# A decoder's latent attention: masking the diagonal blocks of the scores by a VectorE addition in place of TensorE products

## The reference

```python
kv_d = x @ kv_d_w;  q_d = x @ q_d_w
k = concat([(kv_d @ k_u_w), rope(x @ rope_k_w)])       # per head
q = concat([(q_d @ q_u_w), rope(q_d @ rope_q_w)])
v = kv_d @ v_u_w
scores = einsum('bqhd,bkhd->bhqk', q, k) / sqrt(32)
scores = where(tril(ones((256, 256))), scores, finfo.min)
out = einsum('bhqk,bkhd->bqhd', softmax(scores), v)
h = x + out.reshape(b, s, 512) @ o_w
```

## Time and profile before

| what | value |
|---|---|
| time, median of 3 runs | 2256.36 us (2255.92 to 2256.59) |
| profiled execution: its span, the only time shown of it | 2257.6 us |
| PE busy | 2145.6 us, 95% of the span |
| PEld busy | 1788.6 us, 79% |
| DVE busy | 1307.3 us, 58% |
| ACT busy | 1078.4 us, 48% |
| POOL busy | 677.1 us, 30% |

### The profile page before, as it was taken

One profiled execution on the slowest core, in us unless ns is written; L12 is line 12 of the kernel. 1 busy time (PEld: TensorE's weight loads), 2 busy tenths in 40 slices (PEclk: granted clock), 3 DMA queues, 4 the chain that ended last, 5 costly groups with the idle time before them and its releaser, 6 DMA issues. The chain is left out here.

```text
span 2257.6 us, 43111 instructions
## 1 busy us (share of the span) xinstructions
PE 2145.6 (95%) x17918; PEld 1788.6 (79%) x17918; DVE 1307.3 (58%) x2283; ACT 1078.4 (48%) x1887; POOL 677.1 (30%) x684
## 2 busy tenths in 40 slices
PE   6999998899999999999999999999799999899996
PEld 5666666444489999999999999999677877799995
DVE  7666776689854445444544444454555455767764
ACT  4676633478744444333433344333455554425553
POOL 4111210266512221111111111211255543125664
PEclk9999999999999999999999999999999999999998
DMA  7454202100032222321223123221000000258995
GB/s 261 160 170 134 81 11 113 57 1 1 29 131 108 89 100 106 112 75 64 86 94 113 64 87 119 79 70 49 25 2 2 2 2 30 85 187 262 275 274 103
DMA packets 46931, 215.30 MB, mean 95 GB/s; under 512 B 6161, under 2 KB 6161, under 8 KB 32401
## 3 DMA queue, kind: packets, MB, share of 16 engines
q1 hardware_dynamic: 29968, 139.13, 17.1%
q0 software_dynamic: 16768, 73.41, 11.3%
HBM read 169.00 MB, written 43.52 MB: 94 GB/s over the span
## 5 line engine op out<-in xcount | busy, mean ns | idle before, releaser
L336 POOL TENSOR_TENSOR c_prob<-c_prob,c_inv_mass 128x512 f32<-128x512 f32 x128 | 130.5, 1039 | 353.1 <-DVE c_inv_mass L328 353.1
L318 ACT ACTIVATE c_prob<-abc_banks,c_neg_peak 128x256 f32<-128x256 f32 x256 | 117.7, 472 | 178.0 <-DVE c_neg_peak L310 178.0
L50 PE MATMUL abc_banks<-c_ctx,c_wk_hi 128*128 128x256 f32 x512 | 146.6, 286 | 2.3 <-DVE c_qt_lo L2148 2.3
L50 PE MATMUL abc_banks<-bc_xt,bc_wq_hi 128*128 128x256 f32 x512 | 147.7, 288 | 0.0
L51 PE MATMUL abc_banks<-bc_xt,bc_wq_hi 128*128 128x256 f32 x512 | 144.9, 283 | 0.0
L52 PE MATMUL abc_banks<-bc_xt,bc_wq_lo 128*128 128x256 f32 x512 | 144.8, 283 | 0.0
L51 PE MATMUL abc_banks<-c_ctx,c_wk_hi 128*128 128x256 f32 x512 | 143.8, 281 | 0.0
L52 PE MATMUL abc_banks<-c_ctx,c_wk_lo 128*128 128x256 f32 x512 | 143.6, 281 | 0.0
L231 PE MATMUL abc_banks<-ab_wq,b_xqt 128*128 128x512 bf16 x512 | 117.2, 380 | 5.8 <-DVE b_h L202 3.7
L1898 POOL DMA_DIRECT2D c_ctx<-kept_scratch x24 | 13.2, 551 | 347.0 <-PE abc_banks L52 347.0
L3220 POOL DMA_INDIRECT out<-el_r,e_target x44 | 82.8, 1882 | 75.6 <-DMA out<-el_r,e_target 60.6
(11 more groups left out here) (564 smaller groups left out, 7192.4 us busy)
## 6 DMA issues: line engine op xcount, KB each, us to landing
x_res<-b_w SPq DMA_DIRECT2D x48, 512.0 KB, 4.7
bc_xt<-kept_scratch POOLq DMA_DIRECT2D x24, 1024.0 KB, 5.1
c_ctx<-kept_scratch POOLq DMA_DIRECT2D x24, 1024.0 KB, 5.1
e_raw<-e_w SPq DMA_DIRECT2D x15, 1536.0 KB, 9.2
bc_raw<-c_w SPq DMA_DIRECT2D x16, 1024.0 KB, 4.9
h_res<-e_w SPq DMA_DIRECT2D x7, 1536.0 KB, 9.6
kept_scratch<-bc_xt SPq DMA_DIRECT2D x8, 1024.0 KB, 3.9
kept_scratch<-c_ctx SPq DMA_DIRECT2D x8, 1024.0 KB, 3.9
```

The source lines that it names most:

```text
L50: pe.matmul(out, lhs[0], rhs[1], start=first, stop=False)
L318: ins = act.activation(self.prob[:, u % 2, j, :], self.s_ps[:, j, :], ACT.Exp, bias=self.neg_peak[:, u % 2, j:j + 1], accum_out=self.mass[ ...
L336: pool.tensor_tensor(part, part, self.inv_mass[:, u % 2, js].unsqueeze(2).to_broadcast([P, 2, SEQ]), ALU.mult).then_inc(self.prob_done, 1)
```

## The change

The eight mask products of `scores` go, and with them their bf16 operands (`mask` in bf16, `ident_b`), the two casts of DVE that made them, and PE's wait for these. In their place `find_peak` adds the f32 `mask` to the diagonal blocks in `s_ps` with one instruction of 128 x (4 x 2 x 128) elements, in place, and waits for its end (`diagonal_done`) before the first reduction. `s_ready` is now signalled by the last score product.

```diff
@@ -2323,7 +2323,7 @@
         prob = sb("prob", [P, PROBS, 4, CAUSAL])
         ln, shift, ratio = handed.ln, handed.shift, handed.ratio
         rope = sb("rope_sb", [P, 2, TB, RD])
-        mask_f, mask, ident_b = sb("mask_f", [P, P]), sb("mask", [P, P], BF16), sb("ident_b", [P, P], BF16)
+        mask = sb("mask", [P, P])
         junk = sb("junk", [P, D], BF16)
         at_hi, at_lo = handed.xt_hi, handed.xt_lo
         lat_hi, lat_lo = handed.lat_hi, handed.lat_lo
@@ -2353,7 +2353,7 @@
 
         rope_in = sem("rope_in")
         w_in, w_hi_done, w_lo_done = ([sem(f"{n}{k}") for k in range(2)] for n in ("w_in", "w_hi_done", "w_lo_done"))
-        blanked, masked, mask_done = (sem(n) for n in ("blanked", "masked", "mask_done"))
+        blanked, masked, diagonal_done = sem("blanked"), sem("masked"), sem("diagonal_done")
         stats_done, steps, scales_done, y_done, a_done = (sem(n) for n in ("stats_done", "steps", "scales_done", "y_done", "a_done"))
         ring_ready, ring_free = sem("ring_ready"), [sem(f"ring_free{n}") for n in range(BANKS)]
         at_f_done, at_hi_done, at_lo_done, lat_hi_done = (sem(n) for n in ("at_f_done", "at_hi_done", "at_lo_done", "lat_hi_done"))
@@ -2464,10 +2464,10 @@
                 pool.tensor_tensor(o_lo[:, 2 * h:2 * h + 2, :], o_f[:, :, :], f32(o_hi[:, 2 * h:2 * h + 2, :]),
                                    ALU.subtract).then_inc(o_lo_done, 1)
 
-            pool.memset(mask_f[:, :], 0.0).then_inc(blanked, 1)
+            pool.memset(mask[:, :], 0.0).then_inc(blanked, 1)
             pool.memset(neg_peak[:, :, :], 0.0).then_inc(blanked, 1)
             pool.wait_ge(blanked, 2)
-            pool.affine_select(out=mask_f[:, :], in_=mask_f[:, :], compare_op=ALU.is_ge, fill=-1e30, base=0,
+            pool.affine_select(out=mask[:, :], in_=mask[:, :], compare_op=ALU.is_ge, fill=-1e30, base=0,
                                pattern=[[-1, P]], channel_multiplier=1).then_inc(masked, 1)
             pool.wait_ge(rope_in, 16)
             for i in TURNS:
@@ -2580,11 +2580,7 @@
                     for n, (q, k) in enumerate(((qt_hi, kt_lo), (qt_hi, kt_hi), (qt_lo, kt_hi))):
                         for j in range(4):
                             mine = slice(HD * j, HD * (j + 1))
-                            pe.matmul(s_ps[:, j, cols], q[mine, c, tok], k[mine, c, :], start=n == 0, stop=n == 2)
-                for t in range(TB):
-                    for j in range(4):
-                        mm = pe.matmul(s_ps[:, j, 2 * t * P:(2 * t + 1) * P], ident_b[:, :], mask[:, :], start=False, stop=True,
-                                       skip_group_check=True)
+                            mm = pe.matmul(s_ps[:, j, cols], q[mine, c, tok], k[mine, c, :], start=n == 0, stop=n == 2)
                 mm.then_inc(s_ready, 1)
 
             def turned_scores(i, c):
@@ -2693,8 +2689,6 @@
                     turn_inputs(i + 2, 0)
                     turn_inputs(i + 2, 1)
                 if nxt:
-                    if i == -1:
-                        pe.wait_ge(mask_done, 1)
                     scores(i + 1, 0)
                 if i == -1:
                     turn_inputs(1, 0)
@@ -2905,9 +2899,14 @@
                                   ALU.subtract).then_inc(free_of(f"{name}{t}", s), 1)
 
             def find_peak(s, c):
-                dve.wait_ge(s_ready, C * s + c + 1)
+                n = C * s + c
+                dve.wait_ge(s_ready, n + 1)
                 if s > 0:
                     await_ready(dve, "mt", s - 1)
+                diagonal = s_ps[:, :, 0:2 * SEQ].rearrange("p j (b q) -> p j b q", q=P)[:, :, 0::2, :]
+                masks = mask[:, :].unsqueeze(1).unsqueeze(1).to_broadcast([P, 4, TB, P])
+                dve.tensor_tensor(diagonal, diagonal, masks, ALU.add).then_inc(diagonal_done, 1)
+                dve.wait_ge(diagonal_done, n + 1)
                 dve.tensor_reduce(neg_peak[:, 0, c::HD], s_ps[:, :, 0:P], AX.X, ALU.max, negate=True)
                 dve.tensor_reduce(neg_peak[:, 1, c::HD], s_ps[:, :, P:P + SEQ], AX.X, ALU.max, negate=True).then_inc(peak_done, 1)
 
@@ -2951,8 +2950,6 @@
                 dve.tensor_tensor(late.w_lo[:, 0:UP], late.raw[:, 0:UP], f32(late.w_hi[:, 0:UP]), ALU.subtract)
 
             dve.wait_ge(masked, 1)
-            dve.tensor_copy(mask[:, :], mask_f[:, :])
-            dve.tensor_copy(ident_b[:, :], ident[:, :]).then_inc(mask_done, 1)
             dve.wait_ge(rope_in, 16)
             rotate_first(0)
             rotate_first(1)
```

## The result

| | median us (range, runs) | ratio to the kernel before, 95% interval |
|---|---|---|
| before | 2256.14 (2255.68 to 2256.59, 4) | |
| changed | 2275.8 (2270.25 to 2282.45, 4) | 1.0086 [1.007, 1.0101] |
| changed, measured again | 2269.06 (2266.73 to 2282.94, 7) | 1.0068 [1.0045, 1.0091] |

What follows compares the result with a forecast made beforehand. PE was taken as the bound, with the DVE loop right behind it. Losses of 5.5 (five steady turns), 0.94, 1.86 and 1.80 sum to 10.1 us, giving 2266.5 us from 2256.36; range 2261 to 2275, about 0.8.

Steps and rivals of the forecast that it cites:

- the mechanism and the loop: Head groups of scores: PE waits for DVE's reductions before the next group; this loop grows from 3.45 to 4.15 us.
- the reader at 1.03 us: Without mask products, DVE's first reader of the scores starts 1.03 us behind the group's first score product, instead of 1.58.
- the gain on PE: Removing eight mask products for each of 32 groups saves PE 0.43 us a group, 13.8 us in all.
- the turn before batch 0, 1.86 us: Turn already bound by DVE: 0.70 us later twice, 0.24 earlier once, then 0.70 later, together 1.86 us.
- the term without the clock: The 1.86 us loss in the turn before batch 0, from the longer DVE loop at full clock.
- the allowance for the clock: 1 us either way in the forecast range, for where the clock's fall behind the turn before batch 0 lands.
- a falling clock as a rival: New PE idle time before scores and peaks lowers the clock in each of seven turns: 10 us more, 2276; chance 0.07.
- the turn of batch 6, 1.80 us: Last turn with groups of scores: a late addition, longer intervals and 0.70 us more before the transposed peaks, together 1.80 us.
- The statement that all later work only moves with Q: Q is the start of the next turn's queries on PE; the rest of each turn soaks up none of the delay.

Runs made afterwards that it cites:

- the second profile: Profiled execution of the unaltered changed kernel, run again beside other runs of the kernel before: median 2269.06 us, ratio 1.0068.
- the fill ahead alone: Changed kernel plus 5 products with unused results on PE, only ahead of the first scores in the turn before batch 0: 2271.45 us, ratio 1.0059.

## Why the prediction was right and wrong

**Right: the mechanism and the loop.** Each step for the steady turn was found: the reader at 1.03 us, the addition at 1.232 (median of 32, 1205 to 1233 ns), 0.03 for the wait, a loop of 4.17 to 4.19 for 4.15, waits of 0.58 and 0.93 us before groups 1 and 2 where 0.7 to 0.9 were named, a turn of 38.47 for 38.4, the clock 1.00. The rule of the Trainium skill (VectorE: DVE Perf Modes, "The DRAIN you can't avoid") that the semaphore costs nothing between two operations doesn't fit these rows: the reduction L2910 starts 0.03 us behind the addition's end with the wait, and L2911 starts 0.08 us before L2910's end without one. The two pairs are of different operations, and no run leaves out the wait alone, so its own price is not measured.

**Mis-sized: the gain on PE.** 0.43 us a group was read as start to start; leaving the mask out gives 0.37. It changed nothing here, since PE was no longer the bound, but it made the expectation for the version without a mask 2 us too good.

**The step that failed: the turn before batch 0, 1.86 us.** It was worked at a full clock, with "1 us either way for where the clock's fall behind the turn before batch 0 lands". In the trace the fall lands within that turn, and lasts: +6.43 us, of which 5.78 between S0 and the transposed peaks, and 2.74 there in the second profile. Filling PE's idle time brings the clock to 1.00, the period to 4.18, and the difference between S0 and the peaks to 2.07: the term without the clock is right, the allowance for the clock was not. The prediction had a falling clock as a rival, but put it in the steady turns, where PE is idle for some 2 us of 38.5, and argued against it with the waits of 1.03 and 1.17 us in the earlier trace rows. Those rows were the warning: there PE was idle for a third of the loop at 3.45 us, and the change made this longer at just that place (2.1 to 2.3 of 4.15). The right place for the rival was the turn before batch 0, where the loop was the bound already. That this rival's 2276 is so near the measured 2275.8 is luck: it had the clock fall in each steady turn, and there it was 1.00.

**Not shown to have failed: the turn of batch 6, 1.80 us, "and nothing behind it".** The groups are right (+1.83). From the peaks to the stage's end the profile of changed has 2.5 us more than that of before (31.9 against 29.4), and the second one 1.1. But the kernel before, filled in its first turn only, has 31.8 there with the same code, and the changed kernel filled between the groups has 29.4. The statement that all later work only moves with Q took the clock behind it as given; it isn't given in the kernel before either. So the +4.33 of the table is in part a difference between executions. Whether the change makes the low clock there more frequent, these few profiles can't say.

**What stays open.** The two profiled executions of the changed kernel had this stage 17.7 and 11.0 us longer than before. At a full clock the loop accounts for 10.9 of that: 2.07 before batch 0, 1.06 in the turn of batch 0, 5.9 in the five steady ones, and 1.83 in the turn of batch 6. The rest, 6.8 and 0.1, lies at the two ends and goes with the clock there and with the two lengths ahead of S0. How often an execution falls to the one side or the other these profiles can't say. The mean clocks of the runs suggest that most of what the medians have over the loop's share is the clock's, but that is a correlation. With the clock held up in the turn before batch 0, the medians were 12.6 and 12.3 us over those of before (2269.41 less 2256.85, 2267.86 less 2255.52). The four additions of batch 0 cost 8.6 us in the median but 3.3 in that turn of the one execution that was profiled, which was the shortest of the six; no profile shows a longer one. And the stage behind this one took 321.7 to 331.4 us in these profiles with the same code in it. The longest are of filled kernels (331.4, 327.9, 327.8), but another filled one took 322.6, and nothing here says what sets it.

## What to carry to other kernels

Before moving work to an engine that is busy half of the time, count the loop in which one engine waits for the other and back: here that loop had 0.15 to 0.87 us of slack, and 1.25 us went into it against 0.55 that it got back. Price the first and last turns of a pipeline apart, at both levels of the clock, since there the engine that you relieve has less else to do (PE in the turn before batch 0). And ask first whether the work is needed: the mask in the peak pass wasn't, and leaving it out is worth 9 to 10 us, against a loss of 13 to 20 for moving it. As said there, it needs that no left-out score lies so far above the kept ones that their exponentials vanish.

## What the runs showed of the hardware

- With the fill ahead alone, the granted clock was 1.00 up to 1632 and 0.53 over the next 4 us; it fell 1.5 us behind the end of a wait of PE of 2.27 us. In the turn with waits cut to 0.46 to 0.63 us it stayed at 1.00.
- The lower clock lengthens even a loop that another engine bounds: 4.85 us in place of 4.15 to 4.19.
- Useless products made a stretch shorter, 42.37 for 48.36 us, but the same trick did nothing in the last turn (57.86 against 57.76).
- The same code, at the same place, has the clock fall in one execution and not in another: the kernel that masks batch 0 as before had a fall near 1626 that the kernel before itself didn't show, and the changed kernel had the clock back at 1.00 by 1632 in one execution and only near 1643 in the other.
- An addition that reads PSUM and SBUF and writes PSUM in place costs DVE as much as a subtraction from PSUM into SBUF: 1228 and 1225 ns in the mean of 32 for 128x1024 in f32 (L2908, and L382 of the earlier trace rows).
